# The four value-output products between the maxima of the setup, and group 0's first attn blocks by row halves

## The reference

```
x: (8, 100, 128)   ctx_512: (8, 1444, 64)   16 heads of 64
q = layernorm(x) @ Wq;  k = ctx @ Wk;  v = ctx @ Wv
attn = softmax(q k^T * 64**-0.5);  o = (attn v) @ Wo + bo
x = x + tanh(g_xattn) * o
gate, up = fp4_linear(layernorm(x), w_gate), fp4_linear(layernorm(x), w_up)     (352 wide)
x = x + tanh(g_ffn) * fp4_linear(silu(gate) * up, w_down)
```

## Time and profile before

| what | value |
|---|---|
| median of three runs | 548.21 us |
| profiled execution | 547.66 us, its span 545.8 us |
| TensorE busy | 532.4 us (98%) |
| VectorE busy | 439.2 us (80%) |
| ScalarE busy | 312.8 us (57%) |
| chain that ended last | TensorE 91%, VectorE 6% |

### The profile page before, as it was taken

The page is one execution under the profiler, slowest core; times in us unless marked ns, Lnnn a source line. Parts: engine busy times, 40 slices in busy tenths (PEclk is TensorE's granted clock), DMA queues, the critical chain, the costliest instruction groups (busy, mean ns, idle before and its releaser), DMA issues.

```text
span 545.8 us, 8243 instructions
## 1 busy us (share of the span) xinstructions
PE 532.4 (98%) x2769; PEld 319.8 (59%) x2769; DVE 439.2 (80%) x765; ACT 312.8 (57%) x724; POOL 279.9 (51%) x260
## 2 busy tenths in 40 slices
PE   7989999999999999999999999999999999999997
PEld 4655656656565665656566565756556565655553
DVE  5868889798887979798887978789786988877865
ACT  4365546765467556765467645665567654555611
POOL 4046294745629463574927465383826566184300
PEclk9999999999999999999999999999999999999999
DMA  7502001110012100020011100120000200000000
GB/s 186 114 1 56 0 1 31 29 27 2 1 34 37 19 1 28 9 55 0 2 29 35 28 0 2 36 54 1 1 28 4 29 1 1 5 0 1 2 4 4
DMA packets 10017, 12.28 MB, mean 23 GB/s; under 512 B 4144, under 2 KB 7736, under 8 KB 9976
## 3 DMA queue, kind: packets, MB, share of 16 engines
q1 hardware_dynamic: 9000, 8.85, 6.6%
q0 software_dynamic: 560, 2.59, 3.2%
q10 hardware_dynamic: 416, 0.33, 0.2%
HBM read 11.35 MB, written 0.41 MB: 22 GB/s over the span
## 4 chain that ended last, share of the span: by engine, by line
PE 91%; DVE 6%; issue 2%; ACT 1%; POOL 0%; DVEq 0%; ACTq 0%; POOLq 0%
PE attn L931 28%; PE scores L914 19%; PE ring L840 13%; PE scores L915 12%; PE ring L857 5%; PE ring L850 4%; PE ring L820 3%; DVE max L1071 2%; PE ring L863 2%; PE ring L871 1%; PE ring L843 1%; PE attn L887 1%; ACT q_hh L638 1%; DVE e_gate L1025 0%; PE ring L799 0%
## 5 line engine op out<-in xcount | busy, mean ns | idle before, releaser
L749 ACT ACTIVATE probs<-scores 120x400 f32<-120x400 f32 (+1 forms) x384 | 185.5, 505 | 158.5 <-PE scores L915 156.1
L1071 DVE TENSOR_REDUCE max<-ring 116x1 f32<-116x482 f32 (+2 forms) x336 | 203.5, 651 | 58.2 <-PE ring L840 56.7
L592 POOL TENSOR_TENSOR acc_p<-acc_p,probs 120x800 f32<-120x800 f32 x75 | 145.2, 1936 | 64.2 <-ACT probs L749 59.9
L931 PE MATMUL attn<-probs,ctx_n 120*64 120x400 f32 (+1 forms) x768 | 170.2, 524 | 0.6 <-ACT probs L749 0.6
L914 PE MATMUL scores<-q_hh,k_hl 128*120 128x400 f32 (+1 forms) x384 | 154.6, 402 | 1.2 <-DVE q_ls L1075 0.7
L914 PEld LDWEIGHTS scores<-q_hh,k_hl 128*120 128x120 f32 (+1 forms) x384 | 69.6, 181 | 125.1 <-ACT probs L749 89.5
L915 PE MATMUL scores<-q_ls,k_h 71*120 71x400 f32 (+1 forms) x384 | 133.0, 346 | 0.0
L840 PE MATMUL ring<-k_hl,q_hh 128*116 128x482 f32 (+2 forms) x336 | 111.9, 403 | 1.9 <-DVE q_ls L1053 0.7
L915 PEld LDWEIGHTS scores<-q_ls,k_h 71*120 71x120 f32 (+1 forms) x384 | 70.3, 183 | 3.8
L931 PEld LDWEIGHTS attn<-probs,ctx_n 120*64 120x64 f32 (+1 forms) x768 | 38.3, 134 | 53.6 <-issue 33.5
L840 PEld LDWEIGHTS ring<-k_hl,q_hh 128*116 128x116 f32 (+1 forms) x336 | 58.3, 178 | 12.1 <-DVE max L1071 3.0
(11 more groups left out here) (130 smaller groups left out, 473.4 us busy)
## 6 DMA issues: line engine op xcount, KB each, us to landing
ctx_n<-in_ctx SPq DMA_DIRECT2D x8, 360.0 KB
ctxT<-in_ctxT SPq DMA_DIRECT2D x7, 361.0 KB, 4.0
k_hl<-in_ctxT POOLq DMA_DIRECT2D x7, 361.0 KB, 5.0
wvT<-in_WvT SPq DMA_DIRECT2D x2, 256.0 KB, 4.5
wo<-in_L_xattn_Wo SPq DMA_DIRECT2D x1, 512.0 KB, 5.7
x_in<-in_x SPq DMA_DIRECT2D x8, 50.0 KB
out<-y_out SPq DMA_DIRECT2D x8, 50.0 KB
ctxT<-in_ctxT SPq DMA_DIRECT2D x2, 180.5 KB, 3.9
```

The lines of the kernel that those rows point to most:

```text
L592: pool.tensor_tensor(acc_p[0:r, t.g % 2, :], left, probs[0:r, c % PROBS, :], ALU.add).then_inc(sum_p, 1)
L749: act.activation(probs[0:r, c % PROBS, k * HALF:(k + 1) * HALF], scores[0:r, slot % SCORE_BANKS, 0:HALF], ACT.Exp).then_inc(probs_full, 1)
L931: mm = pe.matmul(attn[64 * i:64 * i + C, k, 0:HALF], ctx_n[0:r, par, c, :], probs[0:r, c % PROBS, k * HALF:(k + 1) * HALF], start=(j == 0) ...
L1071: dve.tensor_reduce(max3[0:rows, tile, part:part + 1], src[0:rows, 0:MAXC[part + 1] - MAXC[part]], AX.X, ALU.max).then_inc(free, 1)
```

## The change

- `START`: the maxima of the setup keep their order, but each of the last four has a value-output product ahead of it (0, 1, 2, 3). Before, products 0 and 1 stood behind all twelve maxima, and 2 and 3 in slots 3 and 5 of group 0.
- `FIRST_SLOTS`: the nine remaining maxima stand three in slot 0, one in slot 1, two in each of 2 and 3, and one in slot 4.
- `pv_order` for group 0: the first six pairs go by row halves, the three of half 0 and then the three of half 1. `FIRST_PV_SLOTS` has new slots for them (3, 4, 7 for half 0 and 8, 9, 11 for half 1; before the six stood in 4, 8, 9, 11, 12, 14), and chunks 8 and 9 of half 0 go from slot 21 to 20.
- ScalarE's wait before it writes over an old probs half counts the pairs in the new order, and two waits of TensorE follow the moved products.
- `W_SLOTS`: the first transposes of the quantized weights go from slot 3 to slot 4 of group 2.

```diff
-W_SLOTS = {(2, 3): ('wT', 0), (2, 14): ('wT', 1), ...
+W_SLOTS = {(2, 4): ('wT', 0), (2, 14): ('wT', 1), ...
-FIRST_SLOTS = {0: [('first', 12), ('first', 13)], 1: [('first', 14), ('first', 15)], 2: [('first', 16), ('first', 17)], 3: [('first', 18), ('vo', 2)], 4: [('first', 19), ('first', 20)], 5: [('vo', 3), ('late', 0)], 6: [('q', 0)]}
-FIRST_PV_SLOTS = [4, 8, 9, 11, 12, 14, 16, 18, 21, 22, 24, 26]
+FIRST_SLOTS = {0: [('first', 12), ('first', 13), ('first', 14)], 1: [('first', 15)], 2: [('first', 16), ('first', 17)], 3: [('first', 18), ('first', 19)], 4: [('first', 20)], 5: [('late', 0)], 6: [('q', 0)]}
+FIRST_PV_SLOTS = [3, 4, 7, 8, 9, 11, 16, 18, 20, 22, 24, 26]
...
-START = [("xT", 0), ("A", 0), ("q", 0)] + [("max", _u) for _u in FIRST_MAX] + [("vo", 0), ("vo", 1)]
+START_VO = {8: 0, 9: 1, 10: 2, 11: 3}
+START = [("xT", 0), ("A", 0), ("q", 0)]
+for _n, _u in enumerate(FIRST_MAX):
+    START += [("vo", START_VO[_n])] if _n in START_VO else []
+    START += [("max", _u)]
...
+    if g == 0:
+        return sorted(blocks[:EARLY], key=lambda block: block[1]) + blocks[EARLY:]
...
-                    back = old < 0
-                    act.wait_ge(pv_done, t.count(12, old // 2 * 2 + k + 1))
+                    back = int(old < 0)
+                    act.wait_ge(pv_done, t.count(12, pv_order(t.g - back).index((old % CHUNKS // 2, k)) + 1 - 12 * back))
...
-                        wait_reads(pe, *[(Turn(-1 if part < 2 else 0), ("vo", part)) for part in range(4)], own=bank)
+                        wait_reads(pe, *[(Turn(-1), ("vo", part)) for part in range(4)], own=bank)
...
-                if i == 1 and t.g == 0:
+                if (j, k) == (0, 1) and t.g == 0:
                     pe.wait_ge(second_a_copied, 1)
```

More of the change, by code:

```diff
@@ L76 @@
 LAST_FFN_SLOTS = {**FFN_SLOTS, 20: ('hT', 0), 21: ('hT', 1), 22: ('down', 0)}
-W_SLOTS = {(2, 3): ('wT', 0), (2, 14): ('wT', 1), (2, 15): ('wT', 2), (2, 16): ('wT', 3), (2, 19): ('wT', 4), (2, 20): ('wT', 5)}
+W_SLOTS = {(2, 4): ('wT', 0), (2, 14): ('wT', 1), (2, 15): ('wT', 2), (2, 16): ('wT', 3), (2, 19): ('wT', 4), (2, 20): ('wT', 5)}
 POST_SLOTS = [{7: ('sum', 0), 8: ('proj', 0), 9: ('proj', 1)}, {6: ('sum', 0), 8: ('proj', 0), 9: ('proj', 1)}]
```

## The result

The changed kernel takes 551.13 us (median of 22 runs, 549.73 to 557.07) beside 548.16 for the kernel before in the same comparison (22 runs, 547.02 to 558.48). The ratio is 1.0056, 95% interval 1.0033 to 1.0080. The forecast was 549.2, +1.0 us and no measurable change, in a range of 546.7 to 550.9.

A forecast was written before the change was run, and what follows sets the result against it. TensorE is busy 98% of the span, but VectorE limits the setup and slots 0 to 5. Terms +2.4 - 0.95 + 0 + 0 - 0.45 = +1.0 us gave 549.2 us on the runs' scale, range 546.7 to 550.9.

The forecast's parts named there:

- the sum: All stretches of the change added, +2.4 - 0.95 + 0 + 0 - 0.45 = +1.0 us, no measurable change.
- Setup, +2.4: Setup: four value-output products between the last maxima make TensorE the bound, period 1.35 us; +2.4 us, bounds +1.35 and +2.8.
- Rival 1: Setup hides the four products as the two were hidden: setup +1.35, whole 548.2 us, no change; chance 0.17.
- Slots 0 to 5, -0.95: Group 0: two value-output products leave, one attn pair enters, VectorE decides; late shift 0.95 us earlier, bounds -1.15 and -0.5.
- Slots 6 to 8, 0: Group 0: a second pair moved to slot 7 just fills TensorE's waits for ScalarE; 0, bounds 0 and +0.3.
- Slots 9 to 15, 0: Group 0: two pairs' gain turns into waits for fresh exponentials (0.35, 0.65, 1.0 us); 0, bounds -2.0 and +1.0.
- rival 2: Slots 9 to 15: the two pairs taken away are gained, -2.0 us instead of 0, 547.2 us; chance 0.16.
- rival 3: Slots 9 to 15: ScalarE keeps the first two waits' loss, +1.0 in place of 0, 550.2 us; chance 0.19.
- Slots 20 to 23, -0.45: Group 0: the pair moved from slot 21 to 20 fills TensorE's gaps before scores and shift; -0.45 us, bounds -0.45 and 0.

The follow-up runs named there:

- after: The changed kernel itself, with all the edits, against the kernel before: 551.13 us beside 548.16, ratio 1.0056.
- setup alone: Kernel before with only the four value-output products between the setup's maxima and the nine maxima's new places; attn pairs unmoved: ratio 1.0034, median 552.37 us.
- two between: Kernel before with only its own two setup products moved between the maxima: ratio 1.0061, repeated 1.0043; with three warming products in the wait 1.0029.
- adjacent pairs: Changed kernel with the setup's four value-output products as two adjacent pairs, before the ninth and eleventh maxima: ratio to before 1.0021, median 548.65 us.
- warm in wait: Changed kernel with two warming products in TensorE's wait ahead of the setup's shift product: ratio to before 0.9990, median 549.07 us.
- 128 rows: Changed kernel with value-output products contracting over all 128 rows instead of 64 (output not the reference's): ratio to before 0.9998, median 549.59 us.
- 128 rows, five: Changed kernel with value-output products over all 128 rows and five matmuls each instead of four: ratio to before 1.0041.

## Why the prediction was wrong

*The clock.* The step that failed is the last sentence on what would show it: "A lower clock in the setup would upset every term; TensorE is busier there than before, so I expect none." It had no price in the sum and no chance among the rivals. TensorE was busier by its records (7.19 of 7.40 us up to the last maximum), but with 64-row products each apart. Behind them stood a wait of 1.11 us, which followed from the sum's own order (the last maximum last of all, VectorE's chain behind it) and was not looked at. That stretch at 1.2 GHz costs 1.37 us. It alone put the time outside the range: 551.13 - 1.37 = 549.8.

What brings it down is settled in part. With the 64-row products apart and the wait open, 2 of 54 runs had a mean clock of 0.998 or more (after, setup alone, two between twice). With full rows and the same wait it was 10 of 22, with adjacent pairs 6 of 12, with the wait filled 8 of 12 in the changed kernel and 3 of 12 with two products between. The kernel before had 74 of 113 beside the experiments (17 of 35 to 17 of 21). So the products apart and the open wait together go with the lost clock; no trace with only one of the two has the setup's stretch (warm in wait without the wait; 128 rows and 128 rows, five, without the 64-row products). One trace with both, of two between, lacks it, so a single trace that keeps its clock proves little and the counts carry the reading. How the late stretch, which also lowers a run's mean, divides these counts is open, since only one trace of each kernel shows where it fell.

*Setup, +2.4.* Measured +2.81 (shift 8.92 against 6.11). The term mis-sized is the entry into a value-output product: 0.27 was read behind the second score matmul; behind a maximum it is 0.40 (15.79 to 16.19). 3 x (0.40 - 0.27) = 0.39 is nearly all of the difference of 0.41. The mechanism was right: with four products apart TensorE is the bound of the setup. The Trainium skill ("TensorEngine Tiling (Array Packing)", "Key Properties") says that a change of tiling mode drains TensorE. The trace agrees: the period of 1.49 falls to 1.13 with full rows. Rival 1 (hidden, as the two were) is wrong; even two between the maxima cost 0.63. In adjacent pairs the four cost +1.75 (7.86 against 6.11), where the prediction has +1.35 for products that pack.

*Slots 0 to 5, -0.95.* Measured without the clock, in warm in wait: 8.05 from shift to late shift against 9.09, -1.04. VectorE's reductions decide, as forecast.

*Slots 6 to 8, 0.* 4.99 against 4.97: right.

*Slots 9 to 15, 0.* 8.51 against 8.45: right. The waits of the pairs and of slot 15's scores are in the trace. Of rival 2, two pairs gained, nothing is seen, and rival 3, a loss kept, is not it either: the loss came from elsewhere.

*Slots 20 to 23, -0.45.* Measured -0.30 (10.12 against 10.42 from slot 15 to group 1): the place was right, the size two thirds of it.

*The sum.* Without the clock +1.54 against a forecast of +1.0 to +1.05; with it +2.91, and the medians differ by 2.97. The sign of the sum was right and its size in the traces would have stayed within the 0.3%, by little (1.64 us); the clock took it over.

## What to carry to other kernels

Work put between products that another engine paces is free only up to what that engine leaves: a period of 1.49 us, 0.36 of it changed rows, does not fit beside a reduction of 0.57. Look instead for the waits that stay when all else is in place, here behind the shift product and in slots 6 to 8, and give each a piece of just its length. And where a stretch is rearranged, write down TensorE's longest remaining wait and what stands before it, and put a price on the clock there.

## What the runs showed that was not expected

- Filling a wait with warming products changed nothing in the order of the other work and saved 1.37 us in the trace; taking the warming products away in the kernel before cost nothing in its setup.
- Two products moved between the maxima raised the time about as much as four (1.0061 and 1.0043 in two comparisons, beside 1.0056), though the work behind it moved only 0.63 us; the rest is the clock, 1.4 us for the setup's stretch and 4.6 for the late one, each in one trace.
- Two 64-row products on different halves of the rows take 1.65 us next to each other and 2.2 us apart.
